# Summing pairs of probability tiles on GpSimd: one instruction per head instead of one per two heads

## The reference

```python
mod = (silu(c) @ wmod).reshape(4, 6, 1, -1)          # sa, ca, ga, sb, cb, gb
h = layernorm(x) * (1 + ca) + sa
q, k, v = split((h @ W_qkv + b_qkv) by head);  q, k = rope(q), rope(k)
att = softmax(causal(q @ k.T / sqrt(32)))
x = x + ga * ((att @ v) @ W_proj + b_proj)
h = layernorm(x) * (1 + cb) + sb
x = x + gb * (layernorm(h) * ln_g + ln_b)
```

## Time and profile before

| | |
|---|---|
| time, median of 3 runs | 3445.25 us (3445.21 to 3447.52) |
| profiled execution, its own time | 3444.86 us |
| its span, first to last instruction | 3443.1 us |
| PE busy | 3061.1 us (89%) |
| DVE busy | 2675.1 us (78%) |
| ACT busy | 1762.3 us (51%) |
| POOL busy | 1714.1 us (50%) |
| L510, the pair sums | 360 instructions, 868.3 us busy, mean 2433 ns |
| granted TensorE clock, mean | 0.944 |

### The profile page before, as it was taken

One profiled execution on the slowest core, in us unless ns is written; L12 is line 12 of the kernel. 1 busy time (PEld: TensorE's weight loads), 2 busy tenths in 40 slices (PEclk: granted clock), 3 DMA queues, 4 the chain that ended last, 5 costly groups with the idle time before them and its releaser, 6 DMA issues.

```text
span 3443.1 us, 58785 instructions
## 1 busy us (share of the span) xinstructions
PE 3061.1 (89%) x21664; PEld 1166.0 (34%) x21664; DVE 2675.1 (78%) x4326; ACT 1762.3 (51%) x3411; POOL 1714.1 (50%) x1257
## 2 busy tenths in 40 slices
PE   3799999899989899899998999999888998999895
PEld 1333333334342433424333242433324333242221
DVE  4686777896768788897877878798886878878577
ACT  3416565656645554665544555565544555455451
POOL 2404444563536465473644636465562655636354
PEclk8769999999999999999999999999999999999897
DMA  5302120312031210313113031311203112021022
GB/s 204 98 21 52 31 55 27 83 34 73 13 100 38 72 50 23 93 41 82 38 53 88 25 91 32 81 46 44 77 31 106 44 38 72 26 75 44 24 91 71
DMA packets 180872, 205.25 MB, mean 60 GB/s; under 512 B 21460, under 2 KB 137428, under 8 KB 179428
## 3 DMA queue, kind: packets, MB, share of 16 engines
q1 hardware_dynamic: 180584, 201.50, 20.3%
HBM read 114.09 MB, written 36.50 MB: 44 GB/s over the span
## 4 chain that ended last, share of the span: by engine, by line
PE 44%; DVE 27%; issue 11%; ACT 5%; DVEq 5%; POOLq 3%; POOL 2%; DMA 2%; SPq 1%; ACTq 0%
DVE mpart L872 12%; PE ring L1112 10%; PE ps_out L1162 9%; PE ps_scores L1148 7%; PE ps_den L1179 4%; PE ps_scores L1086 4%; PE ps_den L1185 3%; DVE wk L916 3%; PE ring L1134 3%; DVE dsum L888 2%; ACT xw L660 2%; DVE half L849 2%; DVE wk L914 2%; DVEq L842 2%; DVE x L962 2%
## 5 line engine op out<-in xcount | busy, mean ns | idle before, releaser
L712 ACT ACTIVATE prob<-ps_scores 128x512 f32<-128x512 f32 (+3 forms) x2560 | 1270.1, 538 | 1141.4 <-PE ps_scores L1151 576.2
L872 DVE TENSOR_REDUCE mpart<-ring 128x1 f32<-128x512 f32 (+3 forms) x2560 | 1401.5, 600 | 303.3 <-PE ring L1115 153.3
L510 POOL TENSOR_TENSOR psum<-prob 128x1024 f32<-128x1024 f32 x360 | 868.3, 2433 | 319.0 <-PE ps_den L1179 160.2
L1112 PE MATMUL ring<-qk 96*128 96x512 f16 (+3 forms) x2560 | 894.6, 370 | 127.2 <-DVE mpart L872 115.7
L1148 PE MATMUL ps_scores<-qk 98*128 98x512 f16 (+3 forms) x2560 | 884.4, 359 | 96.5 <-DVE v L854 49.5
L1162 PE MATMUL ps_out<-prob,v 128*32 128x512 f32 (+3 forms) x5120 | 617.5, 555 | 0.0
L1112 PEld LDWEIGHTS ring<-qk 96*128 96x128 f16 x2560 | 240.8, 99 | 982.0 <-DVE mpart L872 713.9
L496 POOL TENSOR_TENSOR xw<-xw,turn 128x512 f32<-128x512 f32 x128 | 203.4, 1589 | 596.4 <-ACT xr L662 553.4
L1148 PEld LDWEIGHTS ps_scores<-qk 98*128 98x128 f16 x2560 | 250.7, 100 | 408.6 <-ACT prob L712 199.8
L1086 PE MATMUL ps_scores<-hT,wg 128*128 128x512 f16 x1536 | 345.1, 381 | 3.5 <-POOL hT L501 3.5
L660 ACT ACTIVATE xw<-ps_scores,bqk 64x512 f32<-64x512 f32 x256 | 175.2, 684 | 300.7 <-PE ps_scores L1086 165.1
(11 more groups left out here) (121 smaller groups left out, 2454.1 us busy)
## 6 DMA issues: line engine op xcount, KB each, us to landing
qk<-half SPq DMA_DIRECT2D x384, 128.0 KB, 3.2
turn<-in_rope_dram SPq DMA_DIRECT2D x64, 512.0 KB, 4.3
xs<-in_L_attn_x_dram SPq DMA_DIRECT2D x124, 256.0 KB, 2.8
attn_out_T<-ot SPq DMA_DIRECT2D x63, 256.0 KB, 2.1
otin<-attn_out_T SPq DMA_DIRECT2D x30, 512.0 KB, 4.7
out_dram<-x SPq DMA_DIRECT2D x60, 256.0 KB, 2.1
wg<-w_qkv_halves SPq DMA_DIRECT2D x16, 768.0 KB, 5.4
qk<-in_L_wmod_dram SPq DMA_DIRECT2D x1, 6144.0 KB, 27.1
```

The source lines that it names most:

```text
L510: pool.tensor_tensor(psum2[:, p], prob[:, s % 3, p], prob[:, (s + 1) % 3, p], ALU.add).then_inc(pair_sum, 1)
L712: act.activation(prob[:, s % 3, p, h % 2, 0:w], ps_scores[(HG * s + h) % NBK][:, 0:w], ACT.Exp, scale=SCALE).then_inc(exp_done, 1)
L872: dve.tensor_reduce(mpart[:, h, qt, kc:kc + 1], ring[n % NBK][:, 0:w], AX.X, ALU.max).then_inc(ring_free, 1)
L1112: mm = pe.matmul(ring[n % NBK][:, 0:w], qk[0:R, G % 2, 0, h, qt * P:(qt + 1) * P], qk[0:R, G % 2, 1, h, kc * QC:kc * QC + w], start=True, ...
```

## The change

Each addition of two heads becomes two additions of one head, 128 x 512, one behind the other. The waits stand ahead of the first, and the semaphore `pair_sum` is raised by the second, so that nobody is told of a sum earlier than at its second half. The elements, their order, the buffers and the other engines' programs stay.

```diff
                 for p in range(2):
                     pool.wait_ge(exp_done, HG * (NS * G + s + 1) + 2 * p + 2)
                     pool.wait_ge(pair_used, wait_value(NP * G + j))
-                    pool.tensor_tensor(psum2[:, p], prob[:, s % 3, p], prob[:, (s + 1) % 3, p],
+                    pool.tensor_tensor(psum2[:, p, 0], prob[:, s % 3, p, 0], prob[:, (s + 1) % 3, p, 0], ALU.add)
+                    pool.tensor_tensor(psum2[:, p, 1], prob[:, s % 3, p, 1], prob[:, (s + 1) % 3, p, 1],
                                        ALU.add).then_inc(pair_sum, 1)
```

## The result

| | before | with halves |
|---|---|---|
| median of the runs compared | 3446.39 us (3445.21 to 3453.01, 4 runs) | 3386.65 us (3381.44 to 3390.52, 4 runs) |
| ratio | 1 | 0.9823, 95% interval 0.981 to 0.9835 |
| span of the profiled execution | 3443.1 us | 3385.4 us |
| granted TensorE clock, mean | 0.944 | 0.954 |

The change makes the kernel 60 us (1.8%) faster. The direction and the mechanism were as predicted; the size was about double (32 us were forecast), and the time lies 1.4 us under the range of 3388 to 3441 us.

The account below looks back on a forecast made before the run. The prediction saw the chain held by DVE's tail operations stalling behind POOL's additions, which made PE wait. From 3444.86 us it took 40 us of gain and added 8 us of cost: 3413 us, range 3388 to 3441 us.

Parts of the forecast that it names:

- The mechanism: Opening analysis: a DVE operation with two SBUF inputs stalls for one POOL addition, not for all that are ready.
- POOL would hold both halves: First rival: POOL does not let DVE in between the halves; 3462 us, slower, chance 0.07.
- DVE's relief: Stall section: DVE's time falls by 36 + 23 + 7 + 1 = 67 us through shorter stalls.
- the three at 1625.19: Stall section: three long L914 waits whose following L916 is free; 1.1 us goes, 0.84 us comes; 1 us in all.
- How much of that reaches the end: Section valuing the relief at the end: 26 + 5 + 9 = 40 us gain, between 19 and 64.
- the idle time for L872: Sign in the changed profile: PE's idle time for these row maxima falls by about 40 us.
- The windows: Gain section: 8 us from each L916's start; PE idle 2.06 us each when stalled, 1.06 when free.
- L962's and L914's shares: Gain section: parts of their relief reaching the end, 9 of 23 us for L962, 5 of 8 for L914.
- The cost: Second-instruction section: later sums, 0.28 us for a pair of steps; half of ACT's 17 us, 8 us, reaches the end.
- all of it comes: Fourth rival: the whole gain of 64 us arrives, less 0 to 4; 3381 to 3390 us, chance 0.08.
- a hidden first part of the stall: Gain section: if the first 0.94 us is hidden, shortening gives back 1.00 us each, 33 us for L916.
- the rival of the late sums: Second rival: longer pair sums reach the end, costing 40 to 50 us; 3445 to 3455 us, chance 0.07.

Follow-up runs that it names:

- the kernels without a clash: Tail's four two-input DVE operations replaced by one-input maxima, second layer norm left out: whole additions 3304.31 us, halves 3313.85 us; kernel before as base.
- the memset: Kernel before, with a 128x48 memset on POOL ahead of each whole addition, making sums late: 3447.39 us, ratio 0.9995.
- the groups without a tail: Kernel before, with halves only in the groups without a tail and whole additions elsewhere: 3453.23 us, ratio 1.0016.
- Quarters: Each addition of two heads in four instructions of 128x256, against the kernel before: 3415.81 us, ratio 0.9905.
- moving the stages: DVE's stages 2 and 4 moved to its step's end, behind the row maxima: whole additions 3370.16 us, halves at the two stages 3366.6 us.

## Why the prediction was wrong, and where it was right

- **The mechanism** (an operation of DVE with two SBUF inputs stands behind one POOL instruction, and comes in at the next boundary) held in every kernel with the clash. L916's long value was 2.69 us at 1024 columns, 1.60 at 512 and 1.06 at 256. The rival that POOL would hold both halves is refuted by L917 at 1021.23.
- **DVE's relief**: 67 us forecast, 59.4 measured. L916 gave 33.3 us (100.1 to 66.8) where I had 36, L962 22.7 (87.3 to 64.6) where I had 23, and L914 6.5 (63.2 to 56.7) where I had 8. L960, which I had left out, takes 4.3 us more (49.6 to 53.9). 36 L916 are stalled now, not 33, as worked out for the three at 1625.19 and their like.
- **The step that failed** is "How much of that reaches the end": the gain of 40 us, worked out from PE's idle time alone. The sum had 40 less 8, 32 us, and the span fell by 57.7. PE's idle time, costs included, fell by 39.9 us, so the term was 8 us too small there. The other 17.8 us are PE's busy time, which I had left out without a reason: the same matmuls took 17.8 us less, with 73 us less at the half clock. (The 40 of the forecast and the 39.9 measured are not the same thing. The first is the gain before costs, and the idle time for L872, of which I had said that it would fall by about 40 us, fell by 51.7.) The windows held the hint. I took their PE column and passed over the granted clock beside it. The falls near a stalled L916 begin 3.4 to 7.2 us from its start and last 3.4 or 6.8 us, so that part of the slow work lay outside of the windows. L962's and L914's shares, taken as 9 and 5, can't be told from L916's by these runs.
- **The cost**: 8 us forecast. It is 9.5 us in the kernels without a clash, nothing with the memset, and some 5 us for the groups without a tail, so the size was about right. The way to it was not: I had ACT's waits for the sums rise from 61.8 to about 80 us, in the same 60 places, and they rose to 122.4 us in 91. What the sums cost in the tail groups of the changed kernel, no run shows by itself.
- **The rival "all of it comes"** (3381 to 3390 us, 0.08) had the right number, in part by luck. Its reason for L916 held: a hidden first part of the stall stays hidden. The 36 stalled L917 have 288.00 - 248.21 = 39.8 us of PE idle in their windows, 1.1 us each, where the earlier trace rows gave 2.06, and the 12 free ones of the tail groups have 96.00 - 83.78 = 12.2 us, 1.0 us each. So a stall of 0.85 us costs PE 0.1 us of idle time, where one of 1.94 us cost 1.00. That would give 30 us, not the 26 I took. But the rival had 64 us from idle time alone, of which 51.7 came before costs; the rest came through PE's busy time, which the rival left out as I did. And the first part is not hidden everywhere, for PE's idle time fell further, from 342.1 to 297.1 us, when the stalls went altogether.
- **Quarters** bore out the rival of the late sums, which was small at halves: it is a matter of dose. Of the lengths tried, with the order left as it was, halves are the fastest.

The windows of the 36 stalled L917, 8 us each from its start, sum, and those of the 12 free ones:

```profile
sum 288.00, PE 248.21 PEld 72.38 DVE 252.72 ACT 135.46 POOL 223.45; mean PE 6.89 PEld 2.01 DVE 7.02 ACT 3.76 POOL 6.21
...
sum 96.00, PE 83.78 PEld 22.35 DVE 92.66 ACT 66.81 POOL 71.21; mean PE 6.98 PEld 1.86 DVE 7.72 ACT 5.57 POOL 5.93
```

Still open: what part of PE's 17.8 us would remain at a constant clock, and how much of the gain of moving the stages is the stalls'.

## What to carry to other kernels

Look for a short instruction whose median is far above its minimum: in this kernel, where POOL and DVE both read two SBUF tensors, each waited for one whole instruction of the other (1.94 us of stall behind 1024 columns, 0.85 behind 512), so long instructions on the less busy engine were paid by the busier one. Shorten them until the wait for their result grows, or move the stalled operation to where nobody waits behind it, which here gave more than the split and cost no instruction. When a stall of PE is valued, add to its idle time what its work behind the stall takes longer, and read the granted clock in the same windows.

## What the runs showed of the hardware

The additions on POOL took 725, 1271, 2359 and 4529 ns in the median for 256, 512, 1024 and 2048 columns: 2.12 to 2.13 us per 1000 columns and 0.18 us for each instruction. That per-instruction part is three times the 60 ns worked out ahead of the result from the Trainium skill's GPSIMD Engine Reference (section Elementwise, side-by-side cycle accounting), and the measurement decides.

The two engines take turns more evenly than the rival feared. The Trainium skill's SBUF page (section Who interferes with whom) has the pair of ports held for a whole instruction by the one issued first; the traces agree on the whole instruction (1.60 us at 512 columns, 2.69 us at 1024). But a queued half without any wait did not come before a DVE operation that already stood waiting: L917 came in at 1022.28, between the L510 and the L511 right behind it.
